# Issuing the eight moves of a unit's keys from ScalarE's queue instead of SyncE's

## The reference

```
for idx in range(LEVELS):
    xa = layernorm(self_attention(xh, ...));  attn_list.append(xa)
    if idx < LEVELS - 1: xh = avgpool4(xa)
for idx in range(LEVELS - 1, 0, -1):
    kv = layernorm(cross_attention(attn_list[idx - 1], kv, ...))
out = layernorm(q + relu(q @ ffn_w1 + b1) @ ffn_w2 + b2)      # then NCHW
y = conv3x3(sign(clip(out)), sign(weight));  result = out + batchnorm(y)
...
```

## Time and profile before

| | us |
|---|---|
| median of 3 runs | 2700.24 (2686.36 to 2701.25) |
| the profiled execution's own time | 2692.97 |
| its span, first to last instruction | 2691.2 |
| PE busy | 2260.2 (84%) |
| DVE busy | 1637.2 (61%) |
| ACT busy | 1420.7 (53%) |
| POOL busy | 1035.6 (38%) |

### The profile page before, as it was taken

How to read it: one execution, slowest core, us unless ns; L and a number is a source line. 1 busy time by engine, 2 the same in 40 slices (tenths; PEclk the granted TensorE clock), 3 DMA queues, 4 the chain that set the end, 5 groups by cost and what they waited for, 6 DMA issues and landing times.

```text
span 2691.2 us, 68616 instructions
## 1 busy us (share of the span) xinstructions
PE 2260.2 (84%) x27032; PEld 1774.8 (66%) x27032; DVE 1637.2 (61%) x5101; ACT 1420.7 (53%) x2531; POOL 1035.6 (38%) x1080
## 2 busy tenths in 40 slices
PE   5887878999799988999799988999799998999700
PEld 4666666777677766777677766777677766777500
DVE  4776665666466665667566665666566655545332
ACT  3654555555366655666466654565456554445332
POOL 3433434443344343444344443444344544443100
PEclk9998999999799999999899998999799999999955
DMA  4553444444244433444244433444334433323077
GB/s 104 130 125 92 122 100 103 109 111 107 75 111 110 110 96 96 109 110 113 77 112 112 109 96 87 112 107 107 82 103 110 112 94 83 80 72 82 19 234 262
DMA packets 387234, 288.26 MB, mean 107 GB/s; under 512 B 61537, under 2 KB 326498, under 8 KB 386914
## 3 DMA queue, kind: packets, MB, share of 16 engines
q1 hardware_dynamic: 386066, 282.88, 40.0%
q10 hardware_dynamic: 848, 0.99, 0.1%
HBM read 69.87 MB, written 56.46 MB: 47 GB/s over the span
## 4 chain that ended last, share of the span: by engine, by line
PE 56%; DVE 17%; SPq 10%; DMA 9%; issue 3%; ACT 3%; POOL 1%; POOLq 0%; ACTq 0%; DVEq 0%
PE ps_y L656 8%; SPq L408 8%; PE ps_hid L645 8%; PE ps_proj L511 6%; PE ps_o L593 5%; PE ps_max L566 4%; PE ps_s L580 4%; PE ps_hid L675 4%; PE ps_s L575 3%; DVE onorm L885 3%; PE ps_y L612 2%; PE ps_y L625 2%; DVE xn L927 2%; PE ps_t L606 2%; SPq L422 2%
## 5 line engine op out<-in xcount | busy, mean ns | idle before, releaser
L1033 POOL TENSOR_TENSOR prob_lo<-prob,prob_hi 128x512 f16<-128x512 f32 x528 | 610.9, 1157 | 931.7 <-ACT prob_hi L744 931.6
L743 ACT ACTIVATE prob<-ps_s 128x512 f32<-128x512 f32 x528 | 315.1, 597 | 403.2 <-PE ps_s L580 401.5
L873 DVE TENSOR_REDUCE negmax<-ps_max 128x8 bf16<-128x512 f32 x528 | 360.3, 682 | 155.9 <-PE ps_max L566 154.5
L880 DVE RECIPROCAL rden<-ps_o 128x8 f32<-128x8 f32 x528 | 108.0, 205 | 548.6 <-PE ps_o L593 547.4
L566 PE MATMUL ps_max<-ks,qs 128*64 128x128 f16 x4224 | 328.2, 288 | 0.3 <-issue 0.2
L885 DVE TENSOR_TENSOR onorm<-ps_o,rden 64x128 f32<-64x128 f32 x1056 | 304.8, 289 | 25.6
L744 ACT ACTIVATE prob_hi<-ps_s 128x512 f16<-128x512 f32 x528 | 313.4, 594 | 0.0
L593 PE MATMUL ps_o<-vb,prob_hi 128*128 128x68 f16 x4224 | 295.1, 197 | 1.6 <-DVE onorm L885 1.6
L656 PEld LDWEIGHTS ps_y<-w_sb,hid 128*128 128x128 f32 x2048 | 266.2, 196 | 33.3 <-issue 28.5
L645 PE MATMUL ps_hid<-xf,w_sb 128*128 128x512 f32 x512 | 283.4, 636 | 3.0 <-ACT yconv L801 2.1
L656 PE MATMUL ps_y<-w_sb,hid 128*128 128x128 f32 x2048 | 277.3, 279 | 0.6 <-ACT hid L782 0.6
(11 more groups left out here) (107 smaller groups left out, 3705.3 us busy)
## 6 DMA issues: line engine op xcount, KB each, us to landing
qs<-q_flat SPq DMA_DIRECT2D x1024, 64.0 KB, 2.5
ks<-k_flat SPq DMA_DIRECT2D x1024, 64.0 KB, 2.7
vb<-v_flat SPq DMA_DIRECT2D x128, 136.0 KB, 2.4
vb<-values_out SPq DMA_DIRECT2D x128, 136.0 KB, 2.8
xin<-in_x SPq DMA_DIRECT2D x64, 256.0 KB, 3.3
self_out<-xa SPq DMA_DIRECT2D x64, 256.0 KB, 2.9
xin<-self_out SPq DMA_DIRECT2D x64, 256.0 KB, 3.3
ffn_out<-x SPq DMA_DIRECT2D x64, 256.0 KB, 2.5
```

What stands on the lines that cost most here:

```text
L743: activation(prob[:, pair_no(u, k) % 2, :], ps_s[:, :], ACT.Exp)
L873: v.tensor_reduce(negmax[:, pair_no(u, k) % 2, :], ps_max[:, :].rearrange("p (a t) -> p a t", t=TOK), AX.X, ALU.max, negate=True).then_inc ...
L1033: g.tensor_tensor(prob_lo[:, i, :], prob[:, i, :], prob_hi[:, i, :], ALU.subtract).then_inc(s_prob, 1)
```

## The change

The function `move_k` goes from SP's block to ACT's block, with its waits, its eight DMAs and its place in the common list; nothing else is different. The DMAs, their sizes, and the semaphore they raise are the same.

```diff
@@ SP's block
-            def move_k(u):
-                if u.kind == "cross":
-                    sp.wait_ge(s_k_taken, u.no + 1)
-                else:
-                    sp.wait_ge(s_proj_lo, proj_no["k", u.seq, None])
-                if same_b[u.seq] is not None:
-                    sp.wait_ge(s_s, last_pair(same_b[u.seq]))
-                for a in range(2):
-                    for w in range(2):
-                        for b in range(2):
-                            r = 64 * a + 32 * w + 16 * b
-                            sp.dma_start(ks[u.b][r:r + 16, :, w, :, :].rearrange("d h t p -> d h (t p)"),
...
-            walk({"load": load, "q_move": move_q, "k_move": move_k, "v_move": move_v, "v_keep": keep_v,
+            walk({"load": load, "q_move": move_q, "v_move": move_v, "v_keep": keep_v,
@@ ACT's block
+            def move_k(u):
+                if u.kind == "cross":
+                    act.wait_ge(s_k_taken, u.no + 1)
+                else:
+                    act.wait_ge(s_proj_lo, proj_no["k", u.seq, None])
+                if same_b[u.seq] is not None:
+                    act.wait_ge(s_s, last_pair(same_b[u.seq]))
+                for a in range(2):
+                    for w in range(2):
+                        for b in range(2):
+                            r = 64 * a + 32 * w + 16 * b
+                            act.dma_start(ks[u.b][r:r + 16, :, w, :, :].rearrange("d h t p -> d h (t p)"),
...
-            walk({"q_hi": q_hi, "k_hi": k_hi, "v_hi": v_hi, "exp": exponentials, "turned": take_turned,
+            walk({"q_hi": q_hi, "k_move": move_k, "k_hi": k_hi, "v_hi": v_hi, "exp": exponentials, "turned": take_turned,
```

More of the change, by code:

```diff
@@ L409, in move_q @@
                                          flat_q(u)[:, w, b, :]).then_inc(s_q_moved[u.b], 16)
-            def move_k(u):
-                if u.kind == "cross":
-                    sp.wait_ge(s_k_taken, u.no + 1)
-                else:
-                    sp.wait_ge(s_proj_lo, proj_no["k", u.seq, None])
-                if same_b[u.seq] is not None:
-                    sp.wait_ge(s_s, last_pair(same_b[u.seq]))
-                for a in range(2):
-                    for w in range(2):
-                        for b in range(2):
-                            r = 64 * a + 32 * w + 16 * b
-                            sp.dma_start(ks[u.b][r:r + 16, :, w, :, :].rearrange("d h t p -> d h (t p)"),
-                                         flat_k(u)[:, a, w, :, :].rearrange("c t p -> c (t p)")
-                                         ).then_inc(s_k_moved[u.b], 16)
             def move_v(u):
@@ L739, in vv_hi @@
                            ).then_inc(s_proj_hi, 1)
+            def move_k(u):
[10 more added lines that the diff above has]
+                            act.dma_start(ks[u.b][r:r + 16, :, w, :, :].rearrange("d h t p -> d h (t p)"),
+                                         flat_k(u)[:, a, w, :, :].rearrange("c t p -> c (t p)")
+                                         ).then_inc(s_k_moved[u.b], 16)
             def exponentials(u, k):
```

## The result

The change makes the kernel slower: 3352.07 us, the median of 4 runs (3350.46 to 3355.07), against 2697.93 for the kernel before on the same chip (2686.36 to 2701.25). The ratio is 1.2436, with a 95% interval of 1.2412 to 1.2461. The profiled execution has a span of 3350.0 us and a mean granted clock of 0.858; before it was 2691.2 and 0.933.

What follows compares the result with a forecast made beforehand. PE's own work was taken to set the time over long stretches, with SP's issues a tenth of the chain. Delays of 598 us, minus 50 gain, plus 110 clock, gave +658 on 2692.97: 3350 us, range 3100 to 3610.

Steps and rivals of the forecast that it cites:

- The argument: On ACT, what stands behind a key burst longer than a pair counts, not the share of ACT's time.
- The burst: Eight key-move issues in a row on ACT, taken as 5.4 us, with 4.4 and 6.5 as ends.
- Place A: Keys of 64 cross units: relu behind the burst ends late, PE's L656 comes 5.65 us later, 362 us.
- Place B: Keys of 48 self units alternating with cross units: exponentials end late, next scores 3.1 us later, 149 us.
- The first stretch: 14 self units with a move behind pairs: exponentials behind the burst delay the scores, 4.5 us each, 63 us.
- the low units: 8 low units: relu behind the burst ends late against L656, taken as 3 us each, 24 us.
- SP's relief: SP loses 136 bursts; PE's waits for `xin` and ACT's for earlier keys shrink: gain 50 us, 0 to 70.
- The clock: Low clock behind the new PE pauses: 85 of them cost 1.3 us each, 110 us, ends 0 and 350.
- The round: A self and a cross unit, eight pairs: from 34.2 us to 45 us.
- A cheap burst: Rival: ACT's burst is at the lower end, 4.4 us, and the clock costs little: 3110 us, chance 14%.
- a faster kernel: Rival: the burst hides on ACT and SP's earlier loads and keys shorten PE's waits: 2640 us, chance 3%.
- The conflict of the bursts: Rival: SP's query and ACT's key bursts lengthen each other: full 4070 us, 5%; partial 3420 to 3490, 12%.

Runs made afterwards that it cites:

- hold5: Kernel before, all moves on SP; ACT only waits at the key move's place until five of the unit's eight query DMAs have landed: 3144.49 us (1.1717).
- spread_load_early: Changed kernel with ACT's key moves in four lumps of two, and input loads due 11.05 instead of 10.3 pairs ahead: 2705.66 us (1.006).
- apart: Changed kernel, with SP's queries of a main unit made to wait until the same unit's keys have landed: 3683.22 us (1.3706).
- load_early: Kernel before, with input loads due 11.05 instead of 10.3 pairs ahead, so SP issues them ahead of the query burst: 2658.88 us (0.9897).
- spread: Changed kernel, all key moves still on ACT but in four lumps of two, about half a pair apart: 2917.6 us (1.0857).

## Why the prediction came out right, and where it was wrong

The time was close (3350 against 3352), and partly by luck: it had PE idle 548 us longer and busy 110 longer (598 - 50 and 110), and the profile has 468 and 191. Two errors of 80 us cancel. The table has the terms beside what the two traces show, summed over the places: how much PE's idle time grew between the end of a pair's scores and the next scores, and how much this interval grew. With the 191 us of longer busy time the idle column makes up the 659.

| term | forecast, us | idle, us | interval, us |
|---|---|---|---|
| 64 places A | 362 | 266 | 287 |
| 48 places B | 149 | 158 | 180 |
| 14 in the first stretch | 63 | 68 | 71 |
| 8 low units | 24 | 13 | 18 |
| together | 598 | 505 | 557 |
| elsewhere (the forecast's gain) | -50 | -37 | |

- **The argument** (a burst is longer than a pair, on an engine asked once a pair) held. `hold5` shows the delay by itself doing it, `spread_load_early` shows the issues without the lump not doing it.
- **The burst**, 5.4 us: near, a mean of 5.61.
- **Place A, 64 x 5.65 = 362: this step failed.** "PE's L656 began at 1212.35, exactly when that relu ended" was a coincidence of two times, and the sentence on L656 under PE's order at place A is wrong too. L656 reads an earlier relu, as L641 at 1499.52 shows. The kernel's own tables say it: in `CROSS` the product `f0` is due at 9.47 and reads the result of `relu0`, due at 8.4, a whole pair earlier; the relu just ahead of it is `relu1`, at 9.4. The row of 1212.35 also has no idle time ahead of it in brackets, so PE had not waited. The slack of 2.39 us, which the prediction named and set aside, was the one that counted. Measured, the 64 places have 266 us of idle time, 96 less than the term, and most of it waits for `prob_hi` (223 us), none for the relu at L641.
- **Place B, 48 x 3.1 = 149**: the right wait, close in size. Of the 158 us, 133 are waits for `prob_hi` and 27 the growth of the wait for `k_image`, for which the forecast had no line.
- **The first stretch, 63, and the low units, 24**: close, one a little small, the other a little large.
- **The last cross units** were priced as place A, and they do show a wait for the relu, at the convolution (L660, 32.3 us in 12 waits, 2.1 before), which has no line in the forecast. Here the burst stands in ACT's order ahead of a relu that is wanted soon:

```profile
2966.76 4.61 ACTq L737 DMA_DIRECT2D ks<-k_flat  x7
...
2972.38 0.69 ACT L782 ACTIVATE hid<-ps_hid,columns_sb 128x512 f32<-128x512 f32 x1
...
2973.22 1.01 PE L660 MATMUL ps_hid<-smap,convs 128*128 128x512 bf16 x2 [4.35 <-ACT hid L782]
```

- **SP's relief, 50**: PE's waits for `xin` lost 12 + 6.6 = 19 us, and 37 us of idle time went away outside the places. ACT's wait for the keys is gone. The keys' last transfer lands 12.1 us behind the scores at place A instead of 14.0, and 11.9 instead of 13.6 at B: some 1.8 us earlier, not 5, since with two queues at work each transfer takes 4.7 us instead of 2.7. The queries' last one lands later, 11.6 us instead of 7.5 at A.
- **The clock, 110: mis-sized.** From the mean clocks, the time at the lower level went from (1 - 0.933) x 2 x 2691 = 361 us to (1 - 0.858) x 2 x 3350 = 951, in 142 falls instead of 43. That is 99 new ones, not 85, and on average each added 190.6 / 99 = 1.9 us of PE's busy time instead of 1.3: the row of before had shown a short one.
- **The round** was forecast at 45 us. The one shown takes 45.0, and the median of the 48 rounds went from 34.6 to 45.1 us.
- **The rivals.** A cheap burst (3110) and a faster kernel (2640) fall with the burst of 5.61. The conflict of the bursts is there in the landings and hardly in the issues: against `apart` the main units' mean burst is 0.27 us longer, some 36 us over 134 bursts. The rule of the Trainium skill beside that rival, page "Perfetto Trace Analysis", section "DMA Instruction — HWDGE (DVE, Sync)", has the generator locked for exclusive use. If that lock is common to these two queues, issues from both at once should lengthen each other; the mean issue of 674 ns against 641 in `apart` bounds that at about 5%.
- **The rule against the change's loss**, page "Perfetto Trace Analysis", section "DMA Optimizations" of the Trainium skill, says that balancing DMAs over the engines may help where descriptor generation is the bottleneck. By it the forecast had 2640 us, and the time is 3352. SP's 10% of the chain did not make it the bottleneck: there was something to gain there, 30 us, and `load_early` takes it without any other engine.

Little stays open. In the changed kernel PE waits for no transfer but the first load, so the conflict of the transfers has no wait of its own there. `hold5`, without it, is 195 us faster against its own kernel before; summed over the 134 places, its exponentials start 194 us sooner behind the scores, and 182 of the 212 us between the two spans lie at these places. I did not separate how the clock and a burst lengthened by the conflict (the 36 us above) share in them.

## What to carry to other kernels

Before a DMA issue is put on an engine that computes, read its order there: how long is the whole lump, what stands right behind it, and how soon is that wanted. The engine's busy share does not answer this: of the 871 gaps of over 0.15 us in ACT's work between the first and the last scores of the kernel before, 16 reached 5 us, and 134 bursts were put in. Cut the lump below the slack (two issues at a time here), or leave it on the engine that computes nothing and reorder that one's queue. And before a wait is priced by two times that touch, follow in the program which result the instruction reads. The list of waits of the kernel before does not replace this: it has the wait for the relu at L656 once and the wait for the exponentials at L575 three times, and only the second one grew.

## What the runs showed of the hardware that I had not expected

- Transfers of two queues at once slow each other down: the same 64 KB moves landed after 4.2 and 4.7 us instead of 2.5 and 2.7, the 256 KB load after 6.2 instead of 3.3. The two queues' packets took 33.9% and 17.5% of 3350 us of the DMA engines' time instead of 40.0% of 2691, 1722 us instead of 1076 for the same packets; in `apart`, with the bursts kept apart, it is 21.0% and 8.1% of 3678, 1070 us again. The Trainium skill, page "DMA: Bandwidth & Descriptors", section "Issuing engines are not separate DMA queues", says that DMAs from all issuers run on the same 16 engines and interleave, and that several issuers save only the time to initiate; with that the landings agree. It adds that this time is usually small relative to the DMA itself. Here one issue takes 0.6 us against a landing of 2.7, but eight in a row take 5.6, and it is the row that ACT stands still for.
- An issue on ACT does not stop the activations already handed over. In `spread`:

```profile
1305.48 0.60 ACT L744 ACTIVATE prob<-ps_s 128x512 f32<-128x512 f32 x1 [2.49 <-PE ps_s L566]
1305.60 0.55 ACTq L738 DMA_DIRECT2D ks<-k_flat  x1
1305.98 0.59 ACT L745 ACTIVATE prob_hi<-ps_s 128x512 f16<-128x512 f32 x1
1306.18 1.19 ACTq L738 DMA_DIRECT2D ks<-k_flat  x1
```

- GpSimd issues the same DMA in about 0.53 us (4.22 for eight), faster than ACT, and in this profile its issues count as busy: 1602.7 us instead of 1035.6, with 1088 of them.
